# Expert stage: first weights addressed in place by a register, second low weights and bias copied, image part written to two halves

## The chip, the cores and the metric

The kernel runs on one core of one Trainium2 chip. The metric is the device time of one execution in microseconds (us), from the chip's own clock. TensorE multiplies matrices (PE in the rows; its weight loads stand apart as PEld, and the instructions that its sequencer runs by itself as PEldq), VectorE is DVE, ScalarE is ACT, GpSimd is POOL, and SyncE (SP) issues the transfers.

## The reference, cut to what matters

The program embeds 32 samples of 25 image and 128 text tokens (153 tokens, 192 channels each), runs a quantized attention, and ends in a layer of experts. Only that last layer is changed. For each sample one of three experts is chosen by a softmax over the token mean; its two products with a gelu between them are added to the residual:

```
B, T, H, F, E = (128, 32, 192, 768, 3)
scores = jax.nn.softmax(jnp.mean(x, axis=1) @ Wg.T, axis=-1)
_, idx = jax.lax.top_k(scores, 1)
h = jax.nn.gelu(jnp.einsum('bth,ehf->betf', x, W1) + b1[None, :, None, :], approximate=False)
y = jnp.einsum('betf,efh->beth', h, W2) + b2[None, :, None, :]
out = jnp.einsum('beth,be->bth', y, w)
```

(The shape line is that of the layer's own draft; here B is 32 samples and T 153 tokens.) The weights are kept as a bf16 high part and a bf16 low part, so that a product in full precision is a sum of several bf16 matmuls.

## The kernel before

`experts` runs one sample per lap, 32 laps, unrolled by four inside a hardware loop (`Fori`), with the first four and the last lap written out ahead of it and behind it. Each engine runs its own program and the engines meet by semaphores.

- **TensorE** (block at L1854). `expert` (L1856) reads the index of the chosen expert from `sel` in SBUF into a register. `first_product` (L1868) makes the hidden layer of sample n: six blocks of 128 hidden units with five matmuls each, 30 matmuls that move 153 columns. `second_product` belongs to the sample one lap before: 18 matmuls of 192 columns for the text tokens (L1879), and 12 of 192 columns for the 25 image tokens (L1884), all into one 64-row place of PSUM. The weights of the second product are addressed by the expert's register as the moving operand.
- **SP** reads the same index (L1827), copies the chosen expert's first weights, high and low, from the tile `vt` (`w1h`, `w1l`) into one of four slots `ws` in the tile `qk` (L1831), and sends finished rows out (L1835, L1839).
- **ScalarE** applies the gelu (L1907), six instructions per lap.
- **VectorE** splits the gelu's result into high and low bf16 parts (`split`, L1936 to L1939), and then, for the sample before, `collect` adds the second bias `b2` of the chosen expert (again by a register, read at L1945), joins the two image halves, and multiplies and adds the residual (L1948 to L1956); every fourth lap one more instruction finishes the image rows (L1961).

The order within a lap on TensorE is: index of the last sample, first product of this sample, second product of the last one.

```
e_last = expert(last[0]) if last is not None else None
if now is not None:
    first_product(now[0], now[1])
if last is not None:
    second_product(last[0], last[1], e_last)
```

Of the kernel before, what the change touches and what calls it, by code (L numbers as in the profile page):

```python
# [7 lines left out]
ALU = mybir.AluOpType  # L8
ACT = mybir.ActivationFunctionType
F32 = mybir.dt.float32  # L10
BF16 = mybir.dt.bfloat16
# [7 lines left out]
P = 128  # L19
B, NI, NT = 32, 25, 128  # L20
N = NI + NT
# [3 lines left out]
C = 192  # L25
# [6 lines left out]
E, FF = 3, 768  # L32
KI = 6
FT = FF // P
# [21 lines left out]
def ds(start, size):  # L56
    return bass.ds(start, size)


class Ctx:  # L60
# [8 lines left out]
    def sb(self, name, shape, dt=F32, stack=None):  # L69
        return (stack or self.stack).enter_context(self.nc.sbuf_tensor(name, shape, dt))  # L70
# [298 lines left out]
def wait_apart(eng, sem, value, passed):  # L369

    eng.wait_ge(sem, value)
    eng.sem_inc(passed, 1)
# [1411 lines left out]
def experts(k, m):  # L1784

    out, Hres = k.d["out"], m["H"]
    X, w1h, w1l, w2h, w2l, sel, gw, gwi, b2, b1s = (m[x] for x in ("X", "w1h", "w1l", "w2h", "w2l", "sel", "gw", "gwi", "b2", "b1s"))
    RING = SLOTS = 4

    HI, BOTH, LO = slice(0, NT), slice(IW, IW + 64), slice(N + 32, N + 32 + NT)  # L1790
    with ExitStack() as st:
        sb = lambda n, s, t=F32: k.sb(n, s, t, st)
        g = m["qkflat"][:, 12288:12288 + 4 * FT * N].bitcast(F32).rearrange("p (u f n) -> p u f n", u=2, f=FT)
        gs = sb("e_gs", [P, 2, FT, N + 32 + NT], BF16)
        ws = m["qkflat"][:, 0:SLOTS * 4 * FF].rearrange("p (s i a f) -> p s i a f", s=SLOTS, i=2, a=2)
        rows_out = m["vi"][:, :, :].rearrange("p a b -> p (a b)").bitcast(F32).rearrange("p (t c) -> p t c", c=C)
        share = m["line"][:, :, :].rearrange("p a b -> p (a b)")[:, 0:2 * FT * B].rearrange("p (e f b) -> p e f b", e=2, f=FT)
        yb, ot, yi, oi = rows_out[:, 0:2, :], rows_out[:, 2:6, :], rows_out[:, 6, :], rows_out[:, 7, :]
        p1, p2, p3 = k.ps("e_p1", [P, 2, 2, 512], F32, st), k.ps("e_p2", [P, 2, 512], F32, st), k.ps("e_p3", [P, 2, 512], F32, st)
        h_acc, h_act, g_hi, g_split, g_room, y_acc, y_bias, y_out, i_half, i_bias, i_out = (  # L1800
            k.sem("e_" + x) for x in ("h_acc", "h_act", "g_hi", "g_split", "g_room", "y_acc", "y_bias", "y_out", "i_half", "i_bias", "i_out"))
        w_in = [k.sem(f"e_w_in{j}") for j in range(SLOTS)]
# [3 lines left out]
        def steps(eng, body):  # L1806

            for kk in range(RING):
                body(0, kk)
            with eng.Fori(1, B // RING) as i:  # L1810
                for kk in range(RING):
                    body(i, kk)
            body(B // RING, 0)

        def batch(c, kk, lag):

            kk -= lag
            if isinstance(c, int) and not 0 <= c * RING + kk < B:
                return None
            return c * RING + kk, kk % RING, c + kk // RING  # L1820

        with k.nc.Block() as block:
            @block.sync
            def _(sp):
                def weights(n, u):

                    e = sp.value_load(sel[0:1, ds(n, 1)], min_val=0, max_val=E - 1)  # L1827
                    if not (isinstance(n, int) and n < SLOTS):
                        wait_apart(sp, h_acc, (n - SLOTS) * 2 + 2, k.passed)
                    for i, w in enumerate((w1h, w1l)):  # L1830
                        sp.dma_start(ws[:, u, i, :, :], w[:, :, e, :]).then_inc(w_in[u], 16)  # L1831

                def rows(n, j, grp):
                    wait_apart(sp, y_out, n + 2, k.passed)
                    sp.dma_start(out[n, NI:N, :], ot[:, j, :]).then_inc(sent[j], 16)  # L1835
                    if j == 3:
                        wait_apart(sp, i_out, grp + 2, k.passed)
                        for q in range(4):
                            sp.dma_start(out[grp * 4 + q, 0:NI, :], oi[32 * q + ID:32 * q + 32, :]).then_inc(image_sent, 16)  # L1839

                def body(c, kk):
                    now, gone = batch(c, kk, 0), batch(c, kk, 4)
                    if now is not None:
                        weights(now[0], now[1])
                    if gone is not None:
                        rows(*gone)
                steps(sp, body)
                for n in range(B - 3, B):
                    rows(n, n % 4, n // 4)
                for q in range(4):  # L1850
                    sp.wait_ge(sent[q], 16 * G + 16)
                sp.wait_ge(image_sent, 64 * G + 64)

            @block.tensor  # L1854
            def _(pe):
                expert = lambda n: pe.value_load(sel[0:1, ds(n, 1)], min_val=0, max_val=E - 1)  # L1856

                def first_product(n, kk):

                    u = kk % 2  # L1860
                    pe.wait_ge(h_act, n * FT + FT)
                    pe.wait_ge(w_in[kk], (n - kk) * 8 + 32)
                    for f in range(FT):
                        o = p1[:, u, f // 3, (f % 3) * N:(f % 3 + 1) * N]
                        fs = slice(f * P, (f + 1) * P)
                        parts = ((0, 0, 0), (1, 0, 0), (0, 0, 1), (0, 1, 2), (1, 1, 2))
                        for a, (w, kt, plane) in enumerate(parts):
                            mm = pe.matmul(o, ws[:, kk, w, kt, fs], X[:, plane, ds(n * N, N)], start=(a == 0), stop=(a == len(parts) - 1))  # L1868
                        if f % 3 == 2:
                            mm.then_inc(h_acc, 1)  # L1870

                def second_product(n, slot, e):
                    pe.wait_ge(g_split, n * 2 + 2)

                    pe.wait_ge(y_bias, n + 1)
                    u = slot % 2
                    parts = [(a, w, f) for f in range(FT) for a, w in ((HI, w2h), (HI, w2l), (LO, w2h))]
                    for b, (a, w, f) in enumerate(parts):
                        mm = pe.matmul(p2[:, u, 0:C], gs[:, u, f, a], w[:, e, f, :], start=(b == 0), stop=(b == 3 * FT - 1))  # L1879

                    wait_apart(pe, i_bias, n + 1, k.passed)
                    parts = [(w, f) for f in range(FT) for w in (w2h, w2l)]
                    for b, (w, f) in enumerate(parts):
                        mm = pe.matmul(p3[0:64, u, 0:C], gs[:, u, f, BOTH], w[:, e, f, :], start=(b == 0), stop=(b == 2 * FT - 1))  # L1884
                    mm.then_inc(y_acc, 1)

                def body(c, kk):
                    now, last = batch(c, kk, 0), batch(c, kk, 1)
                    e_last = expert(last[0]) if last is not None else None
                    if now is not None:  # L1890
                        first_product(now[0], now[1])
                    if last is not None:
                        second_product(last[0], last[1], e_last)
                steps(pe, body)

            @block.scalar
# [14 lines left out]
            def _(v):  # L1911
# [30 lines left out]

                def collect(n, j, grp):
                    u, r = j % 2, slice(32 * j, 32 * j + 32)
                    e = v.value_load(sel[0:1, ds(n, 1)], min_val=0, max_val=E - 1)  # L1945
                    v.wait_ge(y_acc, n + 1)
                    v.wait_ge(y_out, n + 1)
                    v.tensor_tensor(yb[:, u, :], p2[:, u, 0:C], b2[:, e, :], ALU.add).then_inc(y_bias, 1)  # L1948

                    v.wait_ge(i_out, grp + 1)  # L1950
                    v.tensor_tensor(yi[r, :], p3[0:32, u, 0:C], b2[0:32, e, :], ALU.add).then_inc(i_half, 1)  # L1951
                    v.wait_ge(y_bias, n + 3)
                    v.wait_ge(sent[j], (n - j) * 4 + 16)
                    v.scalar_tensor_tensor(ot[:, j, :], yb[:, u, :], gw[:, ds(n, 1)], Hres[:, n, :], ALU.mult, ALU.add).then_inc(y_out, 1)
                    v.wait_ge(i_half, n + 1)
                    v.tensor_tensor(yi[r, :], p3[32:64, u, 0:C], yi[r, :], ALU.add).then_inc(i_bias, 1)  # L1956

                def image(grp):
                    v.wait_ge(i_bias, grp * 4 + 6)
# [3 lines left out]
                def body(c, kk):  # L1963
                    now, last = batch(c, kk, 0), batch(c, kk, 1)
                    if now is not None:
                        split(c, *now[:2])
                    if last is not None:
                        collect(*last)
                        if last[1] == 3:
                            image(last[2])  # L1970
# [129 lines left out]
```

## Time and profile before

| what | value |
|---|---|
| median of 3 runs | 1025.52 us (1023.57 to 1028.31) |
| profiled execution, its own time | 1024.34 us |
| its span, first to last instruction | 1022.5 us |
| TensorE busy over the span | 704.2 us (69%) |
| VectorE busy over the span | 870.8 us (85%) |
| the expert stage | from about 854 us to the end |

The span is what the trace covers; the execution's own time is 1.84 us longer. The shares of busy time are means over stages that have little in common, so the expert stage has to be read by itself. In the trace a matmul's duration contains its way through the array, so that successive matmuls overlap; their distance is read from starts and counts.

### The profile page before, as it was taken

To read this page: it belongs to the slowest core of one execution; us is meant where nothing else is said; L and a number is where in the kernel's file an instruction comes from. 1 tells how busy PE (TensorE), PEld (TensorE's weight loads), DVE (VectorE), ACT (ScalarE), POOL (GpSimd) and SP (SyncE) were. 2 spreads that over 40 slices of the span, in tenths; PEclk is the share of its full clock that TensorE was granted. 3 is DMA by queue.
4 is the path that set the end of the run, shared out by engine and by line. 5 is a ranking of instruction groups with operands and counts; after the bars stand their busy time and mean duration, and the time that the engine had idled before them with its cause. 6 is when DMAs were issued, how large, how long until landed. Compare 5 with 4: busy or idle time off the path is not lost. (4 is left out here: it accounts for less than half of the span.)

```text
span 1022.5 us, 23611 instructions
## 1 busy us (share of the span) xinstructions
PE 704.2 (69%) x6531; PEld 475.1 (46%) x6532; DVE 870.8 (85%) x2388; ACT 709.0 (69%) x1376; POOL 171.0 (17%) x276
## 2 busy tenths in 40 slices
PE   3783387747888467766677756677635384999997
PEld 3562144434655333333344333343323254999896
DVE  6888997888888889999999999999978854677766
ACT  0345365966888799999898999999944393554553
POOL 5851320006665100000000000000005530000000
PEclk9986598988999787789777797777857697999999
DMA  8000000001111111111111111111021004455452
GB/s 259 3 2 0 0 1 1 0 0 37 37 37 37 40 28 25 24 25 28 24 25 24 25 26 24 24 24 24 13 105 64 18 1 155 144 192 199 163 193 90
DMA packets 84272, 54.72 MB, mean 54 GB/s; under 512 B 53704, under 2 KB 83176, under 8 KB 83976
## 3 DMA queue, kind: packets, MB, share of 16 engines
q1 hardware_dynamic: 83208, 54.11, 17.4%
q0 software_dynamic: 1024, 0.13, 0.2%
q8 instruction: 19, 0.31, 0.1%
q14 instruction: 21, 0.17, 0.1%
HBM read 11.90 MB, written 3.76 MB: 15 GB/s over the span
## 5 line engine op out<-in xcount | busy, mean ns | idle before, releaser
L1365 DVE SCALAR_TENSOR_TENSOR expo<-expo,con,pow 128x153 f32<-128x153 f32 x480 | 146.2, 376 | 0.7 <-ACT expo L1275 0.7
L1149 PE MATMUL at_rem<-word,ident_half 128*128 128x459 f16 x160 | 68.7, 430 | 104.6 <-ACT expo L1275 102.5
L1275 ACT ACTIVATE expo<-at_rem,con 128x459 f32<-128x459 f32 x160 | 98.8, 645 | 17.3 <-PE at_rem L1150 13.0
L952 DVE TENSOR_REDUCE rs_ends<-rs_banks 128x770 f32 (+1 forms) x96 | 89.2, 958 | 12.7 <-PE rs_banks L924 10.3
L1401 DVE CUSTOM_DVE_ANT_0 weight_top<-weight_top,line 128x2448 uint16<-128x2448 uint16 x64 | 85.6, 1352 | 6.4 <-ACT line L1267 4.5
L873 ACT ACTIVATE rs_banks<-rs_banks 128x770 f32<-128x770 f32 x96 | 74.3, 796 | 22.9 <-PE rs_banks L916 21.8
L1149 PEld LDWEIGHTS at_rem<-word,ident_half 128*128 128x128 f16 x160 | 15.7, 98 | 152.7 <-ACT expo L1275 146.7
L1238 ACT ACTIVATE word<-at_banks 128x459 uint8<-128x459 f32 x160 | 79.6, 560 | 8.5 <-PE at_banks L779 5.5
L1231 ACT ACTIVATE pT_all<-at_pT 128x768 bf16<-128x768 int16 (+3 forms) x160 | 78.9, 562 | 8.3 <-PE at_pT L1173 2.5
L1907 ACT ACTIVATE qk<-e_p,b1s 128x153 f32<-128x153 f32 x192 | 58.7, 393 | 28.4 <-PE e_p L1868 27.3
L1868 PE MATMUL e_p<-X,qk 128*128 (+1 forms) x960 | 71.8, 234 | 7.3 <-DMA qk<-vt 6.9
L774 PE MATMUL at_banks<-pick,row_top 128*128 128x459 bf16 x160 | 69.9, 437 | 9.3 <-ACT word L1238 8.6
L1267 ACT ACTIVATE line<-weight_top 128x1224 f32<-128x1224 f32 x64 | 74.1, 1159 | 2.8 <-DVE weight_top L1391 2.6
L1868 PEld LDWEIGHTS e_p<-X,qk 128*128 128x128 bf16 x960 | 65.4, 99 | 13.0 <-issue 9.5
L1150 PE MATMUL at_rem<-octave,octave_step 128*128 128x459 f16 x160 | 70.1, 438 | 0.0
L1454 POOL PARTITION_ALL_REDUCE pj_mm<-pj_mm x1 | 0.4, 357 | 406.0 <-DVE pj_mm L1528 406.0
L1391 DVE TENSOR_TENSOR weight_top<-expo,inv_total 128x1224 f32<-128x1224 f32 x64 | 63.2, 1029 | 0.0
L1907 ACT ACT_TABLE_LOAD x16 | 20.5, 1283 | 55.5 <-PE e_p L1868 55.5
L1879 PE MATMUL e_p<-vbd,e_gs 128*128 x384 | 53.1, 246 | 4.1 <-DVE e_gs L1939 4.0
L684 ACT ACTIVATE qi<-pq,biasp,ap 128x306 int16<-128x306 f32 x96 | 48.0, 728 | 11.1 <-PE pq L642 11.1
L1164 PE MATMUL at_pT<-identb,weight_top 128*128 128x128 bf16 x480 | 46.8, 253 | 11.5 <-ACT pT_all L1231 10.2
L779 PE MATMUL at_banks<-kb,qk 128*128 128x153 bf16 x384 | 53.7, 255 | 0.0
(387 smaller groups left out, 2040.7 us busy)
## 6 DMA issues: line engine op xcount, KB each, us to landing
qk<-vt SPq DMA_DIRECT2D x64, 384.0 KB, 3.1
rs_kb<-qk SPq DMA_DIRECT2D x128, 28.7 KB, 1.9
kb<-qk SPq DMA_DIRECT2D x128, 28.7 KB, 1.9
patches<-in_patches SPq DMA_DIRECT2D x4, 768.0 KB
vi<-vt SPq DMA_DIRECT2D x32, 96.0 KB, 2.0
out<-vi SPq DMA_DIRECT2D x32, 96.0 KB, 1.9
pj_w<-in_w SPq DMA_DIRECT2D x1, 2304.0 KB, 8.5
qb<-qk SPq DMA_DIRECT2D x128, 6.0 KB, 1.8
```

The costliest lines, as they stand in the source:

```text
L873: act.activation(banks[:, s, :, 0:5 * W], banks[:, s, 1, 0:5 * W].unsqueeze(1).to_broadcast([P, 2, 5 * W]), ACT.Relu).then_inc(split, 1)
L952: v.tensor_reduce(ends[:, :, n, 5 * b:5 * b + 5], banks[:, slot(u, b), :, 0:5 * W].rearrange("p i (t n) -> p i t n", n=W), AX, ALU.max).th ...
L1149: pe.matmul(out, identh[:, :], bank(word, b).bitcast(F16), start=True, stop=False)
L1150: pe.matmul(out, steph[:, :], bank(oct_, b).bitcast(F16), start=False, stop=True).then_inc(rem_done, 1)
L1231: rank = lambda out, x: act.activation(out, x.bitcast(I16), ACT.Copy, bias=RANKS)
L1238: act.activation(dist[:, 3 * b:3 * b + 3, :], banks[:, b % 3, 0:3 * N].rearrange("p (t n) -> p t n", n=N), ACT.Copy, scale=per_step).then_ ...
L1267: act.activation(flat(line, halves[h]), flat(top, halves[h]), ACT.Copy, scale=LOWER / 3.0, bias=1.5 * LOWER).then_inc(y_done, 1)
L1275: act.activation(bank(ex, b), rem[:, (u + b) % 2, 0:3 * N], ACT.Square, scale=2.0 ** 24, bias=c(5)).then_inc(sq_done, 1)
L1365: ins = v.scalar_tensor_tensor(ex[:, t, :], ex[:, t, :], c(7), pw[:, t, :].bitcast(BF16), ALU.add, ALU.mult, accum_out=tot[:, t:t + 1])
L1401: v.tensor_tensor(flat(top, half).bitcast(I32), flat(top, half).bitcast(I32), flat(line, half).bitcast(I32), ALU.add).then_inc(i_done, 1)
L1868: mm = pe.matmul(o, ws[:, kk, w, kt, fs], X[:, plane, ds(n * N, N)], start=(a == 0), stop=(a == len(parts) - 1))
L1907: act.activation(g[:, u, f, :], p1[:, u, f // 3, (f % 3) * N:(f % 3 + 1) * N], ACT.Gelu, bias=b1s[:, f, ds(n, 1)]).then_inc(h_act, 1)
```

## The change

The first weights are no longer copied: `first_product` takes the stationary operand straight from `w1h` and `w1l`, at the place of the expert that a register holds. SP instead copies the chosen expert's low second weights (`w2l`) and its bias row (`b2`) into four slots `wl` and `bias2`, so that `collect` on VectorE needs no register. The image part is written by alternating matmuls: high weights into rows 0 to 63 of `p3`, low weights into rows 64 to 127, and VectorE adds one more 32-row piece.

```
-        ws = m["qkflat"][:, 0:SLOTS * 4 * FF].rearrange("p (s i a f) -> p s i a f", s=SLOTS, i=2, a=2)
+        bias2 = m["pj_raw"][:, :, :].rearrange("p a b -> p (a b)")[:, 0:SLOTS * C].rearrange("p (u c) -> p u c", u=SLOTS)
+        wl_own = sb("e_w2_low", [P, 2, FT, C], BF16)
...
+        wl = [wl_own[:, 0, :, :], wl_own[:, 1, :, :], wl_line[:, 0, :, :], wl_line[:, 1, :, :]]
...
-                        wait_apart(sp, h_acc, (n - SLOTS) * 2 + 2, k.passed)
-                    for i, w in enumerate((w1h, w1l)):
-                        sp.dma_start(ws[:, u, i, :, :], w[:, :, e, :]).then_inc(w_in[u], 16)
+                        wait_apart(sp, i_bias, n - SLOTS + 3, k.passed)
+                    sp.dma_start(wl[u], w2l[:, e, :, :]).then_inc(w_in[u], 16)
+                    sp.dma_start(bias2[:, u, :], b2[:, e, :]).then_inc(w_in[u], 16)
...
-                def first_product(n, kk):
+                def first_product(n, kk, e):
...
-                    pe.wait_ge(w_in[kk], (n - kk) * 8 + 32)
...
-                            mm = pe.matmul(o, ws[:, kk, w, kt, fs], X[:, plane, ds(n * N, N)], start=(a == 0), stop=(a == len(parts) - 1))
+                            mm = pe.matmul(o, (w1h, w1l)[w][:, kt, e, fs], X[:, plane, ds(n * N, N)], start=(a == 0), stop=(a == len(parts) - 1))
...
                     pe.wait_ge(g_split, n * 2 + 2)
+                    pe.wait_ge(w_in[slot], (n - slot) * 8 + 32)
...
-                    parts = [(w, f) for f in range(FT) for w in (w2h, w2l)]
-                    for b, (w, f) in enumerate(parts):
-                        mm = pe.matmul(p3[0:64, u, 0:C], gs[:, u, f, BOTH], w[:, e, f, :], start=(b == 0), stop=(b == 2 * FT - 1))
+                    for f in range(FT):
+                        pe.matmul(p3[0:64, u, 0:C], gs[:, u, f, BOTH], w2h[:, e, f, :], start=(f == 0), stop=(f == FT - 1))
+                        mm = pe.matmul(p3[64:128, u, 0:C], gs[:, u, f, BOTH], wl[slot][:, f, :], start=(f == 0), stop=(f == FT - 1))
...
-                        first_product(now[0], now[1])
+                        first_product(now[0], now[1], expert(now[0]))
...
-                    e = v.value_load(sel[0:1, ds(n, 1)], min_val=0, max_val=E - 1)
                     v.wait_ge(y_acc, n + 1)
+                    v.wait_ge(w_in[j], (n - j) * 8 + 32)
...
-                    v.tensor_tensor(yb[:, u, :], p2[:, u, 0:C], b2[:, e, :], ALU.add).then_inc(y_bias, 1)
+                    v.tensor_tensor(yb[:, u, :], p2[:, u, 0:C], bias2[:, j, :], ALU.add).then_inc(y_bias, 1)
...
+                    v.tensor_tensor(yi[r, :], p3[32:64, u, 0:C], yi[r, :], ALU.add).then_inc(i_half, 1)
+                    v.wait_ge(i_half, n * 2 + 2)
+                    v.tensor_tensor(yi[r, :], p3[64:96, u, 0:C], yi[r, :], ALU.add).then_inc(i_bias, 1)
```

On TensorE, at the head of a lap inside the loop, the program before has one read of the index (TENSOR_LOAD, with the register instructions that follow it, printed as ISA), and three register instructions of L1868 ahead of the first four of 30 matmuls (`X` is the moving operand, `qk` holds the slots):

```order
L1856 ISA
L1856 TENSOR_LOAD sel
L1856 ISA x2
L1861 ISA
L1868 ISA
L1868 MATMUL e_p<-X,qk 128x153 x2
L1868 ISA
L1868 MATMUL e_p<-X,qk 128x153
L1868 ISA
L1868 MATMUL e_p<-X,qk 128x153 x27
```

At the same place the changed program has two reads of the index, and a register instruction ahead of nearly every matmul, since each block of weights needs its own address (`vt` holds `w1h` and `w1l`); the pattern goes on to the 30th matmul, 25 such instructions in all:

```order
L1859 TENSOR_LOAD sel
L1859 ISA x3
L1859 TENSOR_LOAD sel
L1859 ISA x2
L1864 ISA
L1870 ISA
L1870 MATMUL e_p<-X,vt 128x153
L1870 ISA
L1870 MATMUL e_p<-X,vt 128x153
L1870 ISA
L1870 MATMUL e_p<-X,vt 128x153 x2
```

So 22 register instructions and one read of the index came into the lap of TensorE; the second product keeps its 12 register instructions for 18 matmuls.

On VectorE, `collect` of a lap that is written out ahead of the loop, in the program before (`b` holds the bias rows, `vi` the output rows):

```order
L1945 TENSOR_LOAD sel
L1945 ISA x2
L1948 ISA
L1948 TENSOR_TENSOR vi<-e_p,b 128x192
L1951 TENSOR_TENSOR vi<-e_p,b 32x192
L1954 SCALAR_TENSOR_TENSOR vi<-vi,gw,Hres 128x192
L1956 TENSOR_TENSOR vi<-e_p,vi 32x192
```

And in the changed program (`pj_raw` now holds the copied bias rows):

```order
L1951 TENSOR_TENSOR vi<-e_p,pj_raw 128x192
L1954 TENSOR_TENSOR vi<-e_p,pj_raw 32x192
L1957 SCALAR_TENSOR_TENSOR vi<-vi,gw,Hres 128x192
L1959 TENSOR_TENSOR vi<-e_p,vi 32x192
L1961 TENSOR_TENSOR vi<-e_p,vi 32x192
```

The read of the index and its register instructions are gone from VectorE, and one addition of 32 rows has come in.

## Rows read from the trace of the kernel before

**Rows 1.** Busy time of each engine by stretch of the expert stage:
```profile
core 0: us, PE busy (x) PEld busy (x) DVE busy (x) ACT busy (x) POOL busy (x), PEclk, DMA share, GB/s
...
880.00:900.00 20.00, 19.62 (x248) 17.98 (x246) 13.77 (x31) 10.33 (x29) 0.00 (x0) 1.00 0.50 173
```

**Rows 2.** Chain that ended last, 916 to 926 us: start us, us, what:
```profile
916.51 2.11 PE e_p L1868 x30
918.62 1.49 PE e_p L1879 x18
920.10 1.11 PE e_p L1884 x12
921.21 2.12 PE e_p L1868 x30
```

**Rows 3.** Waits in the stage: who waited for whom, us, times, longest:
```profile
DVE vi L1948 <- issue: 32.2, 28, 1.4
...
PE e_p L1868 <- DMA qk<-vt: 6.9, 1, 6.9
...
PEld e_p L1884 <- issue: 5.0, 32, 0.2
```

**Rows 4.** Timeline of the start: SP's first transfers, first products of two samples:
```profile
853.70 11.84 SPq L1831 DMA_DIRECT2D qk<-vt  x10
...
857.83 5.82 PE L1868 MATMUL e_p<-X,qk 128*128 128x153 bf16 x60 [6.86 <-DMA qk<-vt]
```

**Rows 5.** Timeline of the end: the last sample's first product:
```profile
1008.38 2.20 PE L1868 MATMUL e_p<-X,qk 128*128 x30
```

**Rows 6.** TensorE's sequencer in L1879, 932.4 to 934: count, ns min/median/max, first and last start:
```profile
L1879 PEldq FUSED_REGOPS  x6: 46/46/46, 932.5 to 933.7; - x6
L1879 PEldq ALU_OP  x6: 32/32/32, 932.6 to 933.8; - x6
```

**Rows 7.** The wait behind those matmuls (a helper's line), same stretch:
```profile
L372 PEldq EVENT_SEMAPHORE  x1: 51/51/51, 933.9 to 933.9; - x1
```

**Rows 8.** The same line in an earlier lap, 865 to 866.9, array idle ahead of it:
```profile
L1879 PEldq FUSED_REGOPS  x6: 46/46/46, 865.1 to 866.4; - x6
```

**Rows 9.** L1868 from 930.65 to 931.8, sequencer's register operations:
```profile
L1868 PEldq FUSED_REGOPS  x3: 46/46/46, 930.7 to 931.0; - x3
```

**Rows 10.** L1873, the next sequencer instruction behind all 30 matmuls:
```profile
L1873 PEldq FUSED_REGOPS  x1: 42/42/42, 931.7 to 931.7; - x1
```

**Rows 11.** L1875, the wait ahead of the second product, 930 to 935:
```profile
L1875 PEldq EVENT_SEMAPHORE  x1: 51/51/51, 931.9 to 931.9; - x1
```

**Rows 12.** One read of the index on TensorE, L1856, 929.6 to 930.6:
```profile
L1856 PEldq TENSOR_LOAD <-sel x1: 300/300/300, 929.8 to 929.8; - x1
```

**Rows 13.** L1861, the first instruction behind that read:
```profile
L1861 PEldq FUSED_REGOPS  x1: 46/46/46, 930.5 to 930.5; - x1
```

**Rows 14.** All reads of the index on TensorE in the stage:
```profile
L1856 PEldq TENSOR_LOAD <-sel x32: 298/418/924, 859.3 to 1011.8; - x32
```

**Rows 15.** The loop's branch on TensorE, L1810, once in four laps:
```profile
L1810 PEldq ALU_OP  x1: 32/32/32, 934.1 to 934.1; - x1
...
L1810 PEldq FUSED_REGOPS  x1: 68/68/68, 934.5 to 934.5; - x1
```

**Rows 16.** VectorE by line in the stage: busy us, mean ns, idle before:
```profile
L1956 DVE TENSOR_TENSOR vi<-e_p,vi 32x192 f32<-32x192 f32 x32 | 11.3, 352 | 1.0
```

**Rows 17.** Transfers issued from 880 to 1000 us: KB each, median us to landing:
```profile
qk<-vt SPq DMA_DIRECT2D x49, 384.0 KB, 3.0
```

**Rows 18.** Stretches outside the lap and at its start, columns as in rows 1:
```profile
810.00:845.00 35.00, 28.44 (x178) 16.94 (x176) 23.65 (x97) 32.36 (x87) 12.04 (x12) 1.00 0.00 1
...
560.00:700.00 140.00, 96.60 (x978) 53.58 (x975) 137.53 (x450) 128.49 (x247) 0.00 (x0) 0.81 0.11 24
```

**Rows 19.** First matmuls of the stage, 857.82 to 861:
```profile
L1868 PEld LDWEIGHTS e_p<-X,qk x27: 105/151/152, 857.8 to 861.0; 128*128 128x128 bf16 x27
```

**Rows 20.** The stretch of rows 19, columns as in rows 1:
```profile
857.82:861.00 3.18, 3.17 (x26) 3.18 (x27) 0.00 (x0) 0.92 (x1) 0.00 (x0) 0.50 0.89 324
```

More of the change, by code:

```diff
@@ L1794, in experts @@
         gs = sb("e_gs", [P, 2, FT, N + 32 + NT], BF16)
-        ws = m["qkflat"][:, 0:SLOTS * 4 * FF].rearrange("p (s i a f) -> p s i a f", s=SLOTS, i=2, a=2)
+        bias2 = m["pj_raw"][:, :, :].rearrange("p a b -> p (a b)")[:, 0:SLOTS * C].rearrange("p (u c) -> p u c", u=SLOTS)
+        wl_own = sb("e_w2_low", [P, 2, FT, C], BF16)
+        wl_line = m["line"][:, :, :].rearrange("p a b -> p (a b)")[:, 2 * FT * B:2 * FT * B + FT * C].bitcast(BF16).rearrange("p (u f c) -> p u f c", u=2, f=FT)
+        wl = [wl_own[:, 0, :, :], wl_own[:, 1, :, :], wl_line[:, 0, :, :], wl_line[:, 1, :, :]]
         rows_out = m["vi"][:, :, :].rearrange("p a b -> p (a b)").bitcast(F32).rearrange("p (t c) -> p t c", c=C)
@@ L1944, in collect @@
                     u, r = j % 2, slice(32 * j, 32 * j + 32)
-                    e = v.value_load(sel[0:1, ds(n, 1)], min_val=0, max_val=E - 1)
                     v.wait_ge(y_acc, n + 1)
+                    v.wait_ge(w_in[j], (n - j) * 8 + 32)
                     v.wait_ge(y_out, n + 1)
-                    v.tensor_tensor(yb[:, u, :], p2[:, u, 0:C], b2[:, e, :], ALU.add).then_inc(y_bias, 1)
+                    v.tensor_tensor(yb[:, u, :], p2[:, u, 0:C], bias2[:, j, :], ALU.add).then_inc(y_bias, 1)
                     v.wait_ge(i_out, grp + 1)
-                    v.tensor_tensor(yi[r, :], p3[0:32, u, 0:C], b2[0:32, e, :], ALU.add).then_inc(i_half, 1)
+                    v.tensor_tensor(yi[r, :], p3[0:32, u, 0:C], bias2[0:32, j, :], ALU.add).then_inc(i_half, 1)
                     v.wait_ge(y_bias, n + 3)
@@ L1954, in collect @@
                     v.scalar_tensor_tensor(ot[:, j, :], yb[:, u, :], gw[:, ds(n, 1)], Hres[:, n, :], ALU.mult, ALU.add).then_inc(y_out, 1)
-                    v.wait_ge(i_half, n + 1)
-                    v.tensor_tensor(yi[r, :], p3[32:64, u, 0:C], yi[r, :], ALU.add).then_inc(i_bias, 1)
+                    v.wait_ge(i_half, n * 2 + 1)
+                    v.tensor_tensor(yi[r, :], p3[32:64, u, 0:C], yi[r, :], ALU.add).then_inc(i_half, 1)
+                    v.wait_ge(i_half, n * 2 + 2)
+                    v.tensor_tensor(yi[r, :], p3[64:96, u, 0:C], yi[r, :], ALU.add).then_inc(i_bias, 1)
                 def image(grp):
```

## The prediction

> **What bounds the kernel now.** I began with the stretches of the expert stage, because only that stage is changed. From 880 to 900 us TensorE is busy 19.6 of 20 us at a granted clock of 1.00, its upper level of 2.4 GHz, while VectorE has 13.8 and ScalarE 10.3 us of work [rows 1]. The chain that ended last says the same: there it is a row of TensorE pieces alone, 2.11 us for the 30 matmuls of the first product, 1.49 for the 18 of the text part, 1.11 for the 12 of the image part, and the next lap starts 4.70 us after the last [rows 2]. So the array sets the lap. The waits show how much room the others have: VectorE stands about 1 us per lap at L1948 with nothing to wait for but the instructions in front (32.2 us in 28 cases), which is its read of the index; a transfer is waited for once, 6.9 us at the start; and the first image matmul comes 0.16 us late in each of 32 laps, 5.0 us in all, on "issue" [rows 3]. That last row made me look at TensorE's sequencer, the part that runs register instructions and hands matmuls on.
>
> In L1879, 18 matmuls are handed on with 12 register instructions among them. From the first of these at 932.5 to the wait that stands behind the last matmul at 933.9 it takes 1.4 us [rows 6, 7], so 0.12 us for a register instruction with the one or two matmuls behind it. In a lap where the array stood idle ahead, six of the pairs span 865.1 to 866.4, 0.13 us per step [rows 8]; so the step is the sequencer's own pace. The row's own duration, 46 or 32 ns, is not that pace. Without register instructions matmuls pass much quicker: three register instructions of L1868 are out between 930.7 and 931.0, and L1873, which stands behind 27 more matmuls, runs at 931.7 [rows 9, 10], 0.026 us for a matmul.
>
> A sequencer lap of before, then: first product 1.0 (930.7 to 931.7) [rows 9, 10], the read of the index 0.8 with its offset (a load at 929.8, the next line's instruction at 930.5) [rows 12, 13], second product 1.4 [rows 6, 7], the waits ahead of either product about 0.4 [rows 10, 11], 0.2 behind the wait L372 [rows 7, 15], the loop's branch 0.4 once in four laps [rows 15]. Sum 3.9 us, 0.8 below the array's 4.7. It is hidden by little, and the change goes at just this room.
>
> **The change, part by part.**
>
> *First weights by register, on TensorE.* 22 register instructions come into the first product, 25 in all where 3 were. A step costs 0.12 to 0.13 us; I take 0.125, since these are of the longer kind (46 against 32 ns): 25 x 0.125 = 3.1 us where the array wants 2.1. The bounds: its own duration, 0.046, below; above, 0.026 more if a matmul with a second register costs what a plain matmul does now, so 0.15.
>
> *A second read of the index on TensorE.* 0.7 us from the load to the next line [rows 12, 13], for a load of 300 ns; all loads lie between 298 and 924 ns, with a median of 418 [rows 14]. I take 0.75, so 1.5 for two and 0.1 for the offset; the bounds are 0.7 and 1.3 each. The Trainium skill ("DMA: Bandwidth & Descriptors", Latency and other measured facts) puts a floor of about 600 ns under a `tensor_load`. By that both reads would take 0.2 us more each and the total would be 12 us higher; the trace disagrees, with 298 ns on this engine.
>
> *The new lap.* First product 3.1, two reads 1.6, second product 1.45, waits 0.3 (the new wait on the copied weights is one more register instruction in two of four laps), behind L372 0.2, branch 0.1: 6.75 us. The array's work, 2.1 + 1.5 + at most 1.1, lies inside it. The sequencer becomes the bound, and no semaphore is what TensorE waits for.
>
> *The image part in two halves.* If the two halves of a pair run side by side, 12 matmuls cost 0.55 us instead of 1.11; if not, 1.11. Both lie under the two reads of the next lap, 1.6 us, in which nothing is handed to the array. Worth nothing here; without that cover it would be 0.55 a lap.
>
> *VectorE.* It loses its read of the index, 1.0 us a lap [rows 3], and gains 0.35 us for a fifth small addition [rows 16]. It had slack, and now has a lap of 6.75 us; nothing on the path but the last addition, +0.35 once.
>
> *SP and the transfers.* Before, two copies of 384 KB a lap, 3.0 us to landing [rows 17]; now 288 KB (1152 bf16 in each of 128 partitions) and 96 KB. Their issue waits for `collect` of four samples before, which leaves about three laps, 20 us, to the wait in the second product and VectorE's. Behind it in SP's queue stand only the output rows of that same sample, which wait for the same `collect`. Nothing; if the copy were late, 3 us a lap.
>
> *The start.* The first product no longer waits for a copy. It began at 857.83, while SP issued its first at 853.70 after the same read of the index [rows 4]; so it begins some 3.5 us earlier. But the clock stands at 0.50 there, the 1.2 GHz level, and 26 steps take 3.2 us [rows 19, 20], 3.7 for 30; the second sample's product then goes at the new pace. Its end, 863.65 before (857.83 + 5.82) [rows 4], should come at about 862: -1.7 us.
>
> *The sum.* The last sample's first product ended at 1010.58 (1008.38 + 2.20) [rows 5], 30 laps after 863.65: 146.9 us, 4.90 a lap with all its pauses. Now 30 x 6.75 = 202.5: +55.6. Start -1.7. The tail: image pairs -0.5, less queue on VectorE some tenths, its extra addition +0.35: -0.5. Together +53.4. On the profiled execution's 1024.34 that is 1077.7; the median of the runs is 1.2 us above it, so about 1078.
>
> **The rivals.**
>
> *Faster: register instructions are hidden.* If a step cost under 0.05 us, the sequencer's lap (6.75 - 3.1 + 25 x 0.05 = 4.9) would be no longer than the mean lap now. The array would bound, with 2.1 + 1.5 + 0.55 + 0.1 = 4.25 a lap: 30 x (4.25 - 4.90) - 2.2 = -22, so 1003. For it speaks that the rows give such an instruction 46 ns; against it, both counts of steps. The Trainium skill ("Advanced Engine Details and Errata", Sequencer Loop) says that other engine instructions can be read and queued while a control instruction executes, which would make it so. The trace has the 0.16 us gap ahead of the image part against it [rows 3].
>
> *The clock falls.* TensorE will stand empty for part of each lap. At the lower level the products take 3.7, 3.0 and 1.1 to 2.2 us, 7.8 to 8.9 a lap; held through the stage, 30 x (8.35 - 6.75) = +48, 1126, and a mixture lies between. For it: in the stretch of attention from 560 to 700 us TensorE is busy 97 of 140 us and has a clock of 0.81, so it falls at times. Against it: from 810 to 845 us, in short pieces with 178 matmuls in 35 us, it kept 1.00 [rows 18], and the new lap hands on about 9 a microsecond.
>
> *Slow reads.* If both loads take the longest duration, a lap has 1.1 us more: +34, 1112.
>
> *Two registers in a matmul cost more.* At the bound above, 30 x 25 x 0.026 = +20, 1098.
>
> *A middle price.* At 0.09 us a step: 30 x 25 x -0.035 = -26, 1052.
>
> **How the numbers follow.** Forecast 0.78 (its own range, with steps of 0.12 to 0.13 and reads of 0.7 to 0.85, is 1068 to 1090); middle price 0.04; hidden 0.04; clock 0.05; slow reads 0.04; two registers 0.05. The range must hold 8 in 10: it reaches from the middle price to half-way into slow reads, 1052 to 1106. A change of 0.5% (5 us) is about what a measurement here can tell from none. Only the hidden case lies on the other side: faster 0.04; within 0.5% 0.02, for a step close to 0.05; slower 0.94.
>
> **What would show it.** In the changed trace the sequencer's register instructions on L1870 should number about 800 (25 x 32), with starts 0.12 us apart; a lap should take 6.6 to 6.9 us between first products, and the chain should show "issue" or PE's sequencer between matmuls, not VectorE; the matmuls of L1870 should spread over about 3 us, and TensorE should stand idle for over 1 us behind each image part, with the two reads L1859 in it; VectorE's idle time should have gone over to waits for TensorE; the clock should stay at 1.00. It is wrong if L1870 still takes 2.1 us, if the two loads take much longer than 0.4 us each, or if the clock falls in the stage.

## The result and the profile after

The changed kernel took 1078.02 us (median; 1077.68 to 1081.41), the kernel before 1025.52: a recorded ratio of 1.053, with a 95% interval of 1.0506 to 1.0554 (the two medians by themselves divide to 1.051). One run of the experiment e4 below took 1557.74 us, half as long again as its others, and stands in no median and no ratio of this document. The changed kernel's span is 1076.4 us, 53.9 longer than before.

The same stretch as in [rows 1], by engine (columns as there), shows who lost and who gained time:

```profile
880.00:900.00 20.00, 16.57 (x176) 12.53 (x175) 11.30 (x25) 7.41 (x22) 0.00 (x0) 1.00 0.24 80
```

TensorE is busy 16.57 of 20 us where it was 19.62, with 176 matmuls where there were 248; every other engine has less to do as well, the transfers move half as much, and the clock is 1.00. So every engine waits, and not for the clock or for transfers. The chain that ended last answers to [rows 2] (start us, us, what):

```profile
946.02 3.36 PE e_p L1870 x30
...
951.79 0.88 issue
952.67 3.36 PE e_p L1870 x30
...
958.42 1.36 issue
959.78 3.36 PE e_p L1870 x30
```

The 30 matmuls of the first product are spread over 3.36 us where they took 2.11, and behind the image part stands "issue", time in which TensorE waits for no semaphore: 0.88 us, and 1.36 in the lap with the loop's branch. The lap is 6.65 and 7.11 us here. The waits of the stage (who waited for whom, us, times, longest), beside [rows 3]:

```profile
DVE e_gs L1939 <- ACT qk L1910: 81.6, 32, 4.0
ACT L1910 <- PE e_p L1870: 66.5, 15, 4.9
...
PEld e_p L1870 <- issue: 38.4, 34, 1.8
PE e_p L1870 <- issue: 33.5, 31, 2.9
...
PEld e_p L1886 <- issue: 5.0, 32, 0.2
```

VectorE waits for ScalarE, ScalarE for TensorE's first product, and TensorE for its own instructions. The 32 us that VectorE spent on reading the index are gone, without any use. TensorE's sequencer at L1870 over one lap and over the stage, then its reads of the index at L1859, then the waits and register instructions of the second product (count, ns min/median/max, first and last start):

```profile
L1870 PEldq FUSED_REGOPS  x25: 46/46/79, 945.9 to 949.0; - x25
...
L1870 PEldq FUSED_REGOPS  x796: 46/46/93, 852.6 to 1065.0; - x199
...
L1859 PEldq TENSOR_LOAD <-sel x64: 296/303/568, 851.7 to 1067.2; - x64
...
L1859 PEldq TENSOR_LOAD <-sel x2: 297/298/298, 951.0 to 951.8; - x2
...
L1878 PEldq EVENT_SEMAPHORE  x1: 51/51/51, 949.3 to 949.3; - x1
...
L372 PEldq EVENT_SEMAPHORE  x1: 51/51/51, 950.8 to 950.8; - x1
...
L1864 PEldq FUSED_REGOPS  x1: 42/42/42, 952.4 to 952.4; - x1
```

Each of the 25 register instructions of a lap still lasts 46 ns, as in [rows 9], but from the first to the last it takes 3.1 us: 24 steps of about 0.13 us. The sequencer's lap can be read off: first product 945.9 to 949.2, the waits ahead of the second product to 949.4, second product to 950.8, 0.2 to the first read at 951.0, both reads to 952.4, and the next first product at 952.6. That is 6.7 us without a gap. The start and the end, beside [rows 4] and [rows 5]:

```profile
852.72 4.03 PE L1870 MATMUL e_p<-X,vt 128*128 128x153 bf16 x30 [2.90 <-issue]
857.43 3.36 PE L1870 MATMUL e_p<-X,vt 128*128 128x153 bf16 x30 [0.68 <-ACT qk L1910]
...
1061.99 3.36 PE L1870 MATMUL e_p<-X,vt 128*128 x30 [0.87 <-issue]
```

The second sample's first product ends at 860.79 (863.65 before), the last sample's at 1065.35 (1010.58 before): 204.56 us for 30 laps, 6.82 each, where it was 4.90. Last, the weight loads of the image part's first pairs:

```profile
944.38 0.11 PEld L1886 LDWEIGHTS e_p<-vbd,e_gs 128*64 128x64 bf16 x1
944.38 0.11 PEld L1887 LDWEIGHTS e_p<-e_w_low,e_gs 128*64 128x64 bf16 x1
944.46 0.11 PEld L1886 LDWEIGHTS e_p<-vbd,e_gs 128*64 128x64 bf16 x1
```

The halves of a pair start together, and the pairs follow every 0.08 us: the image part takes about half of its 1.11 us.

### The profile page after: what moved, and what is told of

Its sections match the earlier page's. It is cut to its first block and busy times, and to the rows that moved or that the text cites. A ratio compares the mean times of both kernels' runs of the same rounds, so it can differ in the third digit from the quotient of the medians.

```text
span 1076.4 us, 24304 instructions
## 1 busy us (share of the span) xinstructions
PE 730.5 (68%) x6531; PEld 473.4 (44%) x6532; DVE 882.5 (82%) x2419; ACT 708.4 (66%) x1376; POOL 168.4 (16%) x276
## 5 line engine op out<-in xcount | busy, mean ns | idle before, releaser
L1870 PE MATMUL e_p<-X,vt 128*128 (+1 forms) x960 | 108.0, 239 | 34.3 <-issue 33.5
L1870 PEld LDWEIGHTS e_p<-X,vt 128*128 x960 | 80.3, 98 | 64.2 <-issue 41.7
L1939 DVE CAST e_gs<-qk 128x918 bf16<-128x918 f32 x32 | 20.5, 641 | 81.6 <-ACT qk L1910 81.6
L1882 PE MATMUL e_p<-vbd,e_gs 128*128 x384 | 53.9, 246 | 5.1 <-issue 3.1
```

Of the source, the lines that this page charges most:

```text
L1870: mm = pe.matmul(o, (w1h, w1l)[w][:, kt, e, fs], X[:, plane, ds(n * N, N)], start=(a == 0), stop=(a == len(parts) - 1))
```

## The experiments

The profiled executions begin this stage's first product up to 10 us apart, so beside the medians I compare two lengths of the trace: the **stretch** from the first to the last start of a matmul of the first product (31 laps and one product), and the **tail** from there to the end of the span. The experiments ran in four groups, each with its own runs of the kernel before, whose median went from 1023.26 to 1026.41 us; each experiment's ratio is to those of its group. So kernels of different groups (e1 to e4; e5 to e8; e9 to e11; e12) are compared here by ratio or by stretch.

| kernel | median us | ratio, 95% interval | stretch | tail |
|---|---|---|---|---|
| before | 1025.52 | 1 | 152.5 | 12.2 |
| changed | 1078.02 | 1.053 (1.0506 to 1.0554) | 212.4 | 11.3 |
| e1, one block | 1032.23 | 1.0052 (1.0036 to 1.0068) | 162.7 | 11.5 |
| e6, three blocks' addresses | 1034.44 | 1.0103 (1.0075 to 1.0131) | 169.1 | 11.4 |
| e2, one read in three laps of four | 1068.23 | 1.0404 (1.0384 to 1.0424) | 198.2 | 11.2 |
| e5, e1 and e2 together | 1024.49 | 1.0004 (0.9987 to 1.0022) | 157.3 | 11.8 |
| e3, image part unpaired | 1079.93 | 1.0514 (1.0476 to 1.0551) | 211.6 | 11.4 |
| e4, first weights copied again | 1045.59 | 1.0202 (1.0165 to 1.0238) | 171.3 | 12.2 |
| e7, and in one transfer | 1042.32 | 1.0183 (1.0152 to 1.0214) | 169.5 | 11.6 |
| e8, and output rows from GpSimd | 1033.10 | 1.0084 (1.0057 to 1.0112) | 154.1 | 18.3 |
| e9, and fewer table loads | 1030.73 | 1.005 (1.003 to 1.0069) | 150.1 | 17.9 |
| e12, and tail and read moved | 1015.97 | 0.9917 (0.9896 to 0.9938) | 143.8 | 11.2 |
| e10, before with fewer table loads | 1024.20 | 0.9976 (0.9964 to 0.9988) | 150.8 | 12.2 |
| e11, changed with fewer table loads | 1081.84 | 1.054 (1.0519 to 1.0561) | 211.7 | 11.2 |

**e1 and e6: the register instructions.** The changed kernel, where all six blocks of the first product take their weights from one address (e1, the first edit) or two blocks from each (e6, the second). This leaves out part of the weights: five blocks of six in e1, three of six in e6.

```
-                        fs = slice(f * P, (f + 1) * P)
+                        fs = slice(0, P)
```

```
-                        fs = slice(f * P, (f + 1) * P)
+                        fs = slice(f // 2 * P, (f // 2 + 1) * P)
```

> The changed kernel with all six hidden blocks of the first product reading the first block's weights (five sixths of the first weights are left out): the 30 matmuls still take their weights in place through a register, both reads of the index stay, but only 4 register instructions a lap are left of 25. My theory, that a register instruction costs the sequencer 0.12 us: the sequencer's share of the first product falls from 3.1 to about 1.2 us (4 steps of 0.125 and 26 plain matmuls of 0.026), a lap from 6.8 to about 4.7, the total to about 1013 us (1005 to 1022). Rival, that a matmul whose stationary operand is addressed by a register, or lies in the other tile, is slow by itself: the first product stays at 3.3 us and the total within 5 us of 1078. Rival, that the second read of the index is the cost: no change either, 1078.

> The changed kernel with the weights of three blocks, each used for two successive blocks (half of the first weights left out): 13 register instructions a lap in the first product, both reads as changed. My theory: the sequencer's first product takes 13 x 0.124 + 17 x 0.025 = 2.0 us in place of 3.3, a lap 5.5, the total 1039 us; if the cost per register instruction is the same all the way from 25 down to 4, 1052. Range 1035 to 1055. Rival, that it is not the number of register instructions but that they are there at all: 1070 or more.

The traces count the register instructions on that line, first e1's, then e6's:

```profile
L1870 PEldq FUSED_REGOPS  x156: 46/46/93, 856.1 to 1017.0; - x156
...
L1870 PEldq FUSED_REGOPS  x412: 46/46/93, 851.8 to 1020.2; - x138
```

These are 5 and 13 a lap where the changed kernel has 25 (I had counted 4 for e1). With the number of matmuls and the copies unchanged, 49.7 of the 59.9 us by which the change had lengthened the stretch went with 20 of them. So they are the main cause, and the rival that a step costs nothing is out. So are e1's two: addressed in place by a register all the same, the first product falls to 2.5 us, with both reads of the index still there. But e1 came out at 1032 and not at 1013, outside its range, while e6 lies only 0.5% above it by their ratios, just below its own range. From 25 instructions to 13 the stretch falls by 43 us, from 13 to 5 by 6. Something else holds e1's lap at 5.2 us. Its chain:

```profile
923.20 0.49 issue
923.70 2.48 PE e_p L1870 x30
926.17 1.49 PE e_p L1882 x18
...
928.27 0.46 issue
928.73 2.48 PE e_p L1870 x30
```

The first product is back to 2.5 us, the image part ends 0.6 us after the text part, and then TensorE stands for 0.5 us. Its sequencer in these two laps, at L1870, at the two ends of the waits ahead of the second product, and behind that:

```profile
L1870 PEldq FUSED_REGOPS  x5: 46/51/84, 918.4 to 918.9; - x5
...
L1875 PEldq FUSED_REGOPS  x2: 42/42/42, 919.6 to 924.8; - x2
L1878 PEldq EVENT_SEMAPHORE  x2: 51/51/51, 919.8 to 925.4; - x2
...
L372 PEldq EVENT_SEMAPHORE  x2: 51/51/51, 921.3 to 926.9; - x2
```

First product 918.4 to 919.6, second product to 921.3: 2.9 us, and with the two reads and what stands around them, 1.8 us as in the changed kernel, 4.7. In the second lap the waits take 0.6 us instead of 0.2: the sequencer waits for VectorE's split, which comes after ScalarE's gelu. So e1 seems to be held still by the sequencer, and in part by this loop over ScalarE and VectorE; the array, with 4.6 us of work, is not its bound. No run takes these two apart.

**e2 and e5: the reads of the index.** In e2 a lap hands its index on to the next one instead of reading it again, in three laps of four (the loop's first lap can't). e5 has the edit of e1 as well, and leaves out what e1 does.

```
...
-                    e_last = expert(last[0]) if last is not None else None
+                    e_last = held.pop("e", None)
+                    if e_last is None and last is not None:
+                        e_last = expert(last[0])
...
+                        if kk < RING - 1:
+                            held["e"] = e
```

> The changed kernel, where the second product of a lap keeps the register that the first product of the lap before had read, so that three laps of four have one read of the index in place of two; all else is the same. My theory: each read that goes gives back 0.7 to 0.75 us (0.65 from the load to the next line and 0.1 for its offset), 23 of them 16 to 17 us: about 1061 us (1057 to 1066). Rival, that the read is hidden behind the array's work on the image part: 1078, same. Rival, that the reads are most of the loss: over 35 us faster, below 1043.

> Both earlier edits in one: the changed kernel with the first block's weights for all six blocks (4 register instructions a lap in the first product, five sixths of the first weights left out) and one read of the index in three laps of four. My theory now: with the register instructions gone, what was left over the kernel before was the second read, for which the array's queue of handed-on matmuls does not last (it stood empty 0.4 to 0.9 us behind each image part). A lap of about 4.5 us, about 1018 us (1010 to 1024), below the kernel before. Rival, that something else of the change costs too, such as addresses in the other tile or the paired image part: not below 1026.

The traces count 40 reads in e2 where the changed kernel has 64, 24 fewer and not 23. They shortened the stretch by 14.2 us, 0.59 each, where one read's start lies 0.75 us ahead of the next one's (951.0 and 951.8 above); e2 came out 2 us above its range, and what keeps the rest isn't shown. From e1 to e5 the reads are worth 5.4 us of the stretch and 0.5% of the time, and e5 is level with the kernel before, not below it, just outside its range. So without both, the whole loss is gone. What still holds e5's lap at 5.0 us was not looked into.

**e3: the pairs.** The changed kernel with the image part in one place again, 12 matmuls in a row and no fifth addition.

```
...
-                        mm = pe.matmul(p3[64:128, u, 0:C], gs[:, u, f, BOTH], wl[slot][:, f, :], start=(f == 0), stop=(f == FT - 1))
+                        mm = pe.matmul(p3[0:64, u, 0:C], gs[:, u, f, BOTH], wl[slot][:, f, :], start=False, stop=(f == FT - 1))
...
```

> The changed kernel with the image part's 12 matmuls all into rows 0 to 63, as before, and without the fifth addition on VectorE; weights and copies as changed. My theory: the image part goes back from 0.55 to 1.1 us a lap, under the two reads of the index in which the array stands empty, so 1078 us, same within 2 us. Rival, that the paired image part is worth its 0.55 us a lap here: 17 us slower, 1095.

The stretch is 211.6 against 212.4, and the medians lie within each other's ranges: the half microsecond per lap that the pairs save lies under the reads.

**e4: the other parts of the change by themselves.** First weights copied to slots as before; the copies of the low second weights and of the bias row, and the pairs, as in the changed kernel.

```
...
+                    for i, w in enumerate((w1h, w1l)):
+                        sp.dma_start(ws[:, u, i, :, :], w[:, :, e, :]).then_inc(w_in[u], 16)
...
+                            mm = pe.matmul(o, ws[:, kk, w, kt, fs], X[:, plane, ds(n * N, N)], start=(a == 0), stop=(a == len(parts) - 1))
...
```

> The changed kernel with the first weights copied into slots again, as before the change; the low second weights, the bias row and the paired image part stay as changed. TensorE's sequencer is then back at 3.9 us a lap or less, and the array bounds with 2.1 + 1.5 + 0.55 + 0.1 = 4.25 us a lap in place of 4.90: about 1005 us, faster than both kernels (1000 to 1012). Rival, that the copies, now 1152 KB a lap, become the bound, since the copies of 864 KB and output before took half of the transfer engines' time: a lap of 4.7 us or more, 1018 to 1026. Rival, that copies, bias and pairs are part of the loss: not under 1040.

A clear miss: 1046 where I expected 1005, with a lap of about 5.5 us. A wait for a transfer stands out that the kernel before had only once [rows 3], and the timeline of SP, which issues the transfers (start us, us), shows why:

```profile
PE e_p L1876 <- DMA pj_raw<-b: 25.8, 17, 3.0
```

```profile
929.66 0.66 SPq L1835 DMA_DIRECT2D qk<-vt  x1
930.53 0.52 SPq L1838 DMA_DIRECT2D line<-kb  x1
931.19 0.62 SPq L1839 DMA_DIRECT2D pj_raw<-b  x1
932.09 0.49 SPq L1843 DMA_DIRECT2D out<-vi  x1
933.84 1.49 SPq L1835 DMA_DIRECT2D qk<-vt  x2
...
936.19 0.63 SPq L1839 DMA_DIRECT2D pj_raw<-b  x1
...
937.95 1.70 SPq L1847 DMA_DIRECT2D out<-vi  x4
941.22 1.53 SPq L1835 DMA_DIRECT2D qk<-vt  x2
```

In this stretch SP issues without a wait on any engine, the read of its index in the gaps. Five transfers a lap and four more in every fourth, at 0.5 to 0.9 us each from one to the next, fill its lap; the lap with the four more takes 7.4 us (933.84 to 941.22). That the transfers themselves are not the limit is shown by e8 below, which moves the same copies in a shorter lap. TensorE's granted clock was 0.94 in e4 from 862 to 1031 us, and 0.95 in e7's stage, where the kernel before has 1.00; so part of the miss can be the clock's, and no run takes that apart. The last rival has the number but not the cause: in the changed kernel, which has the low weights, the bias row and the pairs without the copies of first weights, nothing waits for a transfer.

**e7 and e8: relieving SP.** e7 copies high and low first weights in one transfer of 768 KB. e8 also issues the output rows from GpSimd.

```
...
-                    for i, w in enumerate((w1h, w1l)):
-                        sp.dma_start(ws[:, u, i, :, :], w[:, :, e, :]).then_inc(w_in[u], 16)
+                    sp.dma_start(ws[:, u, :, :, :].rearrange("p i a f -> p (i a) f"), w1hl[:, :, e, :]).then_inc(w_in[u], 16)
...
-                    sp.dma_start(out[n, NI:N, :], ot[:, j, :]).then_inc(sent[j], 16)
+                    pool.dma_start(out[n, NI:N, :], ot[:, j, :]).then_inc(sent[j], 16)
...
```

> The kernel with copied first weights, low second weights, bias and pairs, with the two copies of the first weights issued as one. The run with two copies showed SP busy without a pause, some 5.5 us a lap: 0.83 for each copy of first weights, 0.65 and 0.77 for the other two, 0.75 for the output row and about 1 for the index. My theory, that issuing is the bound and not the bytes: the lap falls by one issue, 0.83 us, to about 4.7, the total to about 1020 us (1014 to 1027). Rival, that the bytes are the bound: 1040 or more, same as with two copies.

> The last kernel with the output rows issued from GpSimd's queue, which has no other work in this stage. SP's lap falls to some 3.4 us and the array bounds with 4.25 to 4.4: about 1005 us, faster than the kernel before (998 to 1012). Rival, that the bytes or a later wait bound: as the kernel with one copy or slower. Rival, that GpSimd's own issuing costs more than 4.4 us a lap: slower than that kernel.

Both missed their ranges. One issue less in e7 took 1.8 us off the stretch, and SP's timeline shows why:

```profile
930.71 0.70 SPq L1835 DMA_DIRECT2D qk<-vt  x1
...
932.26 1.25 SPq L1839 DMA_DIRECT2D pj_raw<-b  x1
...
938.10 0.73 SPq L1835 DMA_DIRECT2D qk<-vt  x1
```

The lap with the four image rows takes 7.4 us as in e4 (930.71 to 938.10): the issue of the bias copy now lasts 1.25 us where it lasted 0.63, and the saving is gone. What holds that issue up the trace doesn't show. The rival, that the bytes are the bound, has e7's number, but not e8's. In e8 the stretch fell by 15 us to 154.1, with the same copies and the clock back at 1.00 from 870 to 1020 us, so SP's queue had been a bound; but the tail grew from 11.6 to 18.3 us, and a pause was left behind the image part.

**e9, e10 and e11: the table loads.** ScalarE loads its gelu table once in each pass of its loop, 1.28 us in every second lap. With eight samples in a pass there are 4 loads instead of 16 (and as many fewer branches of that loop, which no run takes apart from the loads). e9 is e8 with this edit, e10 the kernel before with it, e11 the changed one.

```
-                with act.Fori(0, B // 2) as i:
-                    for u in range(2):
-                        n = i * 2 + u
+                with act.Fori(0, B // 8) as i:
+                    for v8 in range(8):
+                        n, u = i * 8 + v8, v8 % 2
```

> The same as e8 (one merged copy of the first weights, output rows issued from GpSimd), and ScalarE's loop takes eight samples per pass instead of two, so that its table load of 1.28 us comes 4 times instead of 16. Theory: e8 stalls on a loop over two laps (first product, table load, six gelus, VectorE's split, second product, index read, first product after next; 9.75 us), in which the table load stands once. 12 loads fewer are worth at most 12 x 1.28 = 15 us; since the array's own work (about 4.3 us a lap) and the index read behind it remain, I expect 1022 us, 1016 to 1029. Rival: the lap is set by the exposed index read on TensorE's sequencer, not by the loop over ScalarE; then it stays at 1033, 1030 to 1036.

> The kernel before with ScalarE's loop taking eight samples per pass, nothing else. Theory: its mean lap of 4.90 us lies 0.2 above the 4.70 of the undisturbed laps, and part of that is the same loop with the table load in it; expect 1021 us, 1016 to 1025. Rival: the array sets the lap and the table load is hidden: 1025.5, within 2 us.

> The changed kernel with ScalarE's loop taking eight samples per pass, nothing else. Theory: a lap of 6.8 us is set by TensorE's sequencer alone, so the table loads are hidden and the time stays at 1078, 1075 to 1081. Rival: the loop over ScalarE contributes there as well, and the time falls by up to 15 us, 1063 to 1073.

e11 is the control: the changed kernel does not gain (a ratio of 1.054 after 1.053, a stretch of 211.7 after 212.4), so the table loads are not on its path. e10 gains 2.2 us, half of what I expected. e9 is a miss: 1030.73 lies in its rival's range and not in its own. It shortens e8's stretch by 4.0 us of at most 15, so the table loads were only the smaller part of what held e8. The pause behind the image part is still in its chain:

```profile
925.60 2.19 PE e_p L1882 x30
...
929.89 0.47 issue
930.37 2.25 PE e_p L1882 x30
...
934.71 0.84 issue
```

and the read of the index (on L1870 in e9's program), which lies in it, has become slow, a median of 794 ns where the changed kernel has 303:

```profile
L1870 PEldq TENSOR_LOAD <-sel x29: 299/794/1093, 859.9 to 996.6; - x29
```

**e12: a version that beats both.** e9 with two edits: the last rows issued from SP again, and the read of the index behind the first product.

```
...
-                    e_last = expert(last[0]) if last is not None else None
...
-                        second_product(last[0], last[1], e_last)
+                        second_product(last[0], last[1], expert(last[0]))
...
+                for n in range(B - 3, B):
+                    rows(sp, n, n % 4, n // 4, end_sent)
```

> e9 with two edits: the output rows of the last three samples and the last image rows are issued from SP and no longer from GpSimd, and TensorE reads the index behind the first product instead of ahead of it. Theory: in e8 and e9 the program ends 17.9 to 18.3 us after the last first product against 12.2 in the kernel before, because GpSimd's last transfers land late; this gives back about 6 us (1030.7 to about 1025). And the gap of 0.4 to 0.9 us behind e9's image part is the read of the index, which the short paired image part no longer covers; behind 30 handed-on matmuls that the array needs 2.2 us for, it is covered, and the lap falls from 4.78 to about 4.45 us: 10 us more. Together 1014, 1008 to 1022. Rival: the read in its new place holds up the second product instead, or the loop over ScalarE and VectorE sets the lap; then only the tail is gained, 1025, 1022 to 1028.

1015.97 us, 0.9917 of the kernel before (0.9896 to 0.9938), and as expected. The trace tells the two edits apart, if neither reaches into the other's part: the stretch is 6.3 us shorter than in e9, the tail 6.7. Its chain, its stretch by engine, and a wait of the text part from 870 to 1000 us (us, times, longest):

```profile
914.94 2.17 PE e_p L1884 x30
917.11 1.52 PE e_p L1895 x18
...
919.25 2.12 PE e_p L1884 x30
```

```profile
920.00:940.00 20.00, 19.49 (x271) 17.35 (x268) 16.02 (x37) 10.47 (x31) 4.37 (x8) 1.00 0.84 294
```

```profile
PE e_p L1895 <- issue: 2.9, 10, 0.4
```

The next first product follows the image part without a pause, this lap is 4.31 us, and with TensorE busy 19.5 of 20 us the array is nearly the bound again. The mean lap is 4.57 us: in some laps the moved read now delays the text part, 0.29 us each in ten of the laps of that window, where in e9 TensorE stood 10.0 us on "issue" ahead of its first product in 18. Here the half microsecond that a pair saves should count; e12 without pairs was not run.

## Why the prediction was right, step by step

The forecast was 1078 us, and it came out at 1078.02. The mechanism was right; that the numbers agree so closely is luck. The prediction's own working adds up to 1024.34 + 53.4 + 1.2 = 1078.9, which it rounds down, and its terms were off by +2.0, -1.2 and -0.4 us. Two of its bounds don't follow from their terms either: steps of 0.12 to 0.13 and reads of 0.7 to 0.85 us give 1071 to 1088 and not 1068 to 1090, and half-way into slow reads is 1095, not 1106.

- **That the sequencer becomes the bound: shown.** 796 register instructions, about 800 forecast; starts about 0.13 us apart; "issue" between TensorE's groups; and e1, e2 and e5 take the loss away with those instructions and reads, with the same number of matmuls.
- **First product, 25 steps of 0.125, 3.1 us: mis-sized by a little.** The 24 steps between first and last instruction take 3.1 us, and with the matmul behind the last one the next instruction comes after 3.3. A step costs about 0.13 us where the row prints 46 ns. The Trainium skill ("Advanced Engine Details and Errata", Sequencer Loop) lets other engine instructions be read and queued while a control instruction executes; no such cover shows here, since a step is longer than the 46 ns of the one and the 0.026 us of a plain matmul [rows 9, 10] together.
- **Two reads, 1.6 us: too high.** 951.0 to 952.4 is 1.4 us. The loads have a median of 303 ns and not 418. Both errors nearly cancel: 6.7 us on an undisturbed lap and 6.82 in the mean, against 6.75. 30 laps cost +57.6 us, 55.6 forecast.
- **The start, -1.7 us: it was -2.86** (860.79 against 863.65); about 1 us of that was there when the stage began. The first product ran at a granted clock of 0.50 from 852.72 to 856.08, the 1.2 GHz level, as forecast, and took 4.03 us where 3.7 were forecast.
- **The clock, a rival with a chance of 0.05: it stayed at 1.00** from 857 to 1075 us in the changed kernel's trace. It did not in two others of the same kind: 0.99 in the mean of e11's stage (860 to 1060 us) and 0.98 in e2's (860 to 1052 us), each with stretches at 0.50; e11's stretch is no longer for it.
- **The tail, -0.5 us: it was -0.9** (11.0 against 11.9 from the end of the last first product). The three terms, +57.6 - 2.86 - 0.87, are the span's 53.9.
- **Image part, SP and VectorE, each at nothing: shown by e3 for the pairs.** For VectorE the fifth addition takes 354 ns, and it has 81.6 us of waits. SP's copies land after 2.4 and 2.0 us, and nothing waits for them.
- **A pause of over 1 us behind each image part: 0.88 to 1.36**, about 1.0.
- **One reading of the profile was wrong without harm.** I took the 0.16 us ahead of the image part for a mark of the sequencer. It is 5.0 us in 32 cases in both kernels, though their sequencers' laps differ by 2.8 us, so it doesn't come from that lap. The Trainium skill ("TensorEngine Tiling (Array Packing)", Key Properties) says that a change of the tiling mode drains TensorE; the text part is 128*128 and the image part 128*64, which fits. No run took the change of mode away.

The expectations of the experiments fared worse than the prediction, by one idea used too freely: that a lap is the longer of two sums, the array's (about 4.6 us in e1) and the sequencer's (for which I had taken too little). In the laps read off above the sequencer takes one thing after another; while it waits for the split or reads an index, no matmul is handed to the array, and a short image part doesn't cover that. e12 shows in the kernel with copies that placing decides: behind 30 matmuls that are already handed on, the same read leaves 2.9 us of pauses from 870 to 1000 us where e9 had 10.0, and the stretch is 6.3 us shorter. e4 failed on a term that I had not priced at all, SP's issuing, and e7 on taking the duration of an issue for fixed: the bias copy's went from 0.63 to 1.25 us. How e1's 0.5 us above its sequencer's 4.7 divide between the branch, the split and longer reads stays open; the changed kernel with its reads moved was not tried.

## What to carry to other kernels

An operand addressed by a register was not free on TensorE in this kernel: count the register instructions of a lap, price them by the distance between their starts, not by their printed duration, and compare the sum of the sequencer's lap with the array's. A change that takes work from one engine (VectorE's read, the copies' bytes) is worth nothing when it puts a tenth of a microsecond on each of 22 steps of the engine whose sequencer then sets the lap. And a stall that only the sequencer sees, such as a read into a register, belongs behind the longest run of matmuls without register instructions.

## What the runs showed of the hardware

- **A register instruction and the matmul behind it** take about 0.13 us, 24 steps in 3.1 us, at a granted clock of 1.00; matmuls without one pass the sequencer in 0.026 us [rows 9, 10].
- **A read of the index into a register is slower in kernels that move more beside it:** a median of 303 ns in the changed kernel (74 to 80 GB/s in the stage), 418 in the kernel before [rows 14] and 794 in e9 (273 GB/s). But it doesn't follow the rate alone: e10, with the copies of the kernel before, has a median of 306. That the transfers are the cause is likely, and not shown.
- **The program ends later when GpSimd issues its last transfers.** In e9 its last four issues stand here, and the span ends at 1026.4; in e12 SP's last four end 1.5 us ahead of the end at 1013.9:

```profile
1017.46 2.02 POOL L1855 DMA_DIRECT2D out<-vi  x4 [0.70 <-DVE vi L1974]
```

```profile
1011.05 1.36 SPq L1835 DMA_DIRECT2D out<-vi  x4
```

From the last issue's end it is 6.9 us with GpSimd and 1.5 with SP. Earlier in the stage GpSimd's rows land after 2.9 us, so what the program does in its last microseconds is not all transfer; the trace doesn't show what.
